# Attention scores per head over four PSUM banks, with VectorE masking all tiles but the first

## The reference, cut to what matters

```python
def xattn(Q, ctx):                          # Q = layernorm(x)
    q, k, v = heads(Q @ Wq.T), heads(ctx @ Wk.T), heads(ctx @ Wv.T)
    s = einsum('nhqd,nhkd->nhqk', q, k) / sqrt(32)
    s = where(padding_mask, s, -inf); s = where(attention_mask, s, -inf)
    a = softmax(s); a = where(isnan(a), 0, a)
    return einsum('nhqk,nhkd->nhqd', a, v).reshape(n, s, 512) @ Wo.T
x = x + xattn(layernorm(x), ctx_1024)
x = x + (layernorm(x) @ W[idx].T + b[idx])  # idx: one expert for each of the 256 positions
```

## Time and profile before

| | |
|---|---|
| median of 3 runs | 872.61 us (872.24 to 873.02) |
| the profiled execution's own time | 871.33 us |
| its span, from first to last instruction | 869.5 us |
| PE busy | 843.0 us, 97% |
| DVE busy | 697.8 us, 80% |
| POOL busy | 630.0 us, 72% |
| ACT busy | 434.9 us, 50% |
| granted TensorE clock, mean | 0.99 of full speed |

### The profile page before, as it was taken

How to read it: one execution, slowest core, us unless ns; L and a number is a source line. 1 busy time by engine, 2 the same in 40 slices (tenths; PEclk the granted TensorE clock), 3 DMA queues, 4 the chain that set the end, 5 groups by cost and what they waited for, 6 DMA issues and landing times. The chain is left out here.

```text
span 869.5 us, 19093 instructions
## 1 busy us (share of the span) xinstructions
PE 843.0 (97%) x6509; PEld 676.7 (78%) x6510; DVE 697.8 (80%) x1021; ACT 434.9 (50%) x762; POOL 630.0 (72%) x826
## 2 busy tenths in 40 slices
PE   8999999999999999999999999999993999999996
PEld 6778887778878888778877888777762788888885
DVE  5988888788888888788888888788778877777774
ACT  5655556565755556555756556555465222222221
POOL 3798778686768668686768668685675677777774
PEclk9999999999999999999999999999996999999998
DMA  9613342524252442524243442522488899999993
GB/s 341 226 43 92 116 136 74 171 74 136 74 157 88 135 135 74 170 77 136 74 154 95 132 133 76 162 83 77 141 270 283 256 282 293 291 281 290 286 293 110
DMA packets 123130, 141.70 MB, mean 163 GB/s; under 512 B 16128, under 2 KB 89376, under 8 KB 120992
## 3 DMA queue, kind: packets, MB, share of 16 engines
q1 hardware_dynamic: 108656, 99.45, 36.5%
q0 software_dynamic: 11360, 35.66, 12.8%
q10 hardware_dynamic: 3024, 5.45, 2.2%
HBM read 90.18 MB, written 51.90 MB: 163 GB/s over the span
## 5 line engine op out<-in xcount | busy, mean ns | idle before, releaser
L1827 PE MATMUL pA<-wf_hl,x_hi 128*128 x560 | 139.2, 391 | 1.8 <-DVE wf_hl L356 1.1
L1827 PEld LDWEIGHTS pA<-wf_hl,x_hi 128*128 128x128 f32 x560 | 105.4, 189 | 24.3 <-issue 2.6
L1111 POOL TENSOR_TENSOR s<-s,row 128x1024 f32<-128x1024 f32 x64 | 121.8, 1903 | 3.1 <-DVE row L1371 3.1
L1768 ACT CAST x_hi<-x2t 128x512 fp32r<-128x512 f32 x70 | 43.5, 621 | 147.1 <-PE pA L1827 136.4
L1519 PE MATMUL pS<-wo_hi,ot_hi 128*128 128x512 f32 x256 | 106.9, 418 | 0.3 <-DVE ot_lo L1375 0.3
L1087 POOL TENSOR_SCALAR y_mom<-y_mom 128x1 f32<-128x1 f32 x64 | 15.9, 248 | 124.9 <-DVE y_mom L1392 123.8
L1519 PE MATMUL pS<-xt_hi,wq_hi 128*128 128x512 f32 x256 | 105.3, 411 | 0.2 <-DVE wq_lo L1412 0.2
L1222 ACT CAST ot_hi<-pA 128x512 fp32r<-128x512 f32 x64 | 37.6, 587 | 128.9 <-PE pA L1622 128.8
L1519 PE MATMUL pS<-wo_lo,ot_hi 128*128 128x512 f32 x256 | 100.9, 394 | 0.0
L1519 PE MATMUL pS<-wo_hi,ot_lo 128*128 128x512 f32 x256 | 100.8, 394 | 0.0
L1519 PE MATMUL pS<-xt_lo,wq_hi 128*128 128x512 f32 x256 | 100.6, 393 | 0.0
(11 more groups left out here) (134 smaller groups left out, 1937.6 us busy)
## 6 DMA issues: line engine op xcount, KB each, us to landing
xq<-x_scratch SPq DMA_DIRECT2D x280, 64.0 KB
xt_raw<-in_x_t SPq DMA_DIRECT2D x16, 1024.0 KB, 6.9
x<-in_x SPq DMA_DIRECT2D x64, 256.0 KB, 3.2
y_scratch<-y_biased SPq DMA_DIRECT2D x64, 256.0 KB, 2.1
x_scratch<-y_normal SPq DMA_DIRECT2D x64, 256.0 KB, 2.9
wf_hl<-in_wf ACTq DMA_DIRECT2D x5, 1024.0 KB, 6.1
ctx_raw<-in_ctx_t SPq DMA_DIRECT2D x32, 128.0 KB, 3.0
wf_hl<-in_wf SPq DMA_DIRECT2D x3, 1024.0 KB, 8.7
```

The lines of the kernel that those rows point to most:

```text
L1111: pool.tensor_tensor(p, p, h.row[:, t % h.c, 3, :].unsqueeze(2).broadcast_to([P, H, BK]), ALU.mult)\
L1827: return pe.matmul(pA[:, r % 2, :], rows[:, r % 2, c * P:(c + 1) * P], w, start=first, stop=last)
```

## The change

Scores are now made head by head. A product takes 32 rows (one head), all 128 positions as weights and the 64 keys of that head; sixteen of them replace the eight. Head `4j + m` sits on rows `32j` to `32j + 31` and goes to bank 2 + j, so that four row groups write four banks. These are 256 columns in each of banks 2 to 5 (`pF`), and thus overlap what is now the second half of `pS` and both banks of `pT`; the projections move to banks 0 and 1. As scores and transposes share banks 4 and 5, PE gets two new waits: `scores(t)` waits for `p_copied` of tile t-2, and `transpose_p(t)` waits until DVE has drained the scores of tile t+1. `kd` loses its zeros, its two memsets and seven of the eight copies of `kt_copy`. Only tile 0 is masked on PE. `scores(t+2)` stands after `project_o(t-1)` in all steps, and in step 0 after the first piece of Q. Three idle products follow `weigh_v` in steps 59 to 62. The route's placing product moves from `pT` to `pA`, since scores now take `pT`'s bank.

```diff
-        self.pe_masks = (0, 1) + tuple(range(self.tiles - 5, self.tiles))
+        self.pe_masks = (0,)
...
-    def scores_late(self, t):
-        return t < self.tiles - 7
-
-    def scores_first(self, t):
-        return self.tiles - 7 <= t < self.tiles - 2
+    def has_scores(self, t):
+        return t < self.tiles - 2
...
-        pS = top.enter_context(nc.psum_tensor("pS", [P, 2, 2 * 512], F32))
-        pT = top.enter_context(nc.psum_tensor("pT", [P, 2, 512], F32))
-        pA = top.enter_context(nc.psum_tensor("pA", [P, 2, 512], F32))
+        banks = top.enter_context(nc.psum_tensor("banks", [P, 8, 512], F32))
+        pS = banks[:, 0:4, :].rearrange("p (r b) n -> p r (b n)", r=2)
+        pT = banks[:, 4:6, :]
+        pA = banks[:, 6:8, :]
+        pF = banks[:, 2:6, 0:HG * BK].rearrange("p j (m k) -> p j m k", m=KC)
...
-        h.kd = sb("kd", [P, 2, h.nb, KC, 2 * BK], F32, st)
+        h.kd = sb("kd", [P, 2, h.nb, KC, BK], F32, st)
...
-            pool.memset(h.kd[:, 1], 0.0).then_inc(zeroed, 1)
...
             def kt_copy(g):
-                if g == 0:
-                    act.wait_ge(zeroed, 2)
                 act.wait_ge(kt_done, g + 1)
-                for j in range(HG):
-                    r = slice(j * DH, (j + 1) * DH)
-                    src = bank("KT", g)[r, :].rearrange("p (c s k) -> p c s k", c=KC, s=2)
-                    for s in range(2):
-                        ins = act.copy(h.kd[r, g % 2, s, :, (j % 2) * BK:(j % 2 + 1) * BK], src[:, :, s, :])
-                ins.then_inc(kt_copied, 1)
+                act.copy(h.kd[:, g % 2], bank("KT", g).rearrange("p (c s k) -> p s c k", c=KC, s=2)).then_inc(kt_copied, 1)
...
-            dve.memset(h.kd[:, 0], 0.0).then_inc(zeroed, 1)
...
-                    if h.scores_first(t):
-                        mask_scores(t + 2)
...
-                    if h.scores_late(t):
+                    if h.has_scores(t):
                         bias_scores(t + 2)
                     ot_low(t)
-                    if h.scores_late(t):
+                    if h.has_scores(t):
                         shift_biased(t + 2)
...
             def scores(t):
                 g, q = divmod(t, h.c)
                 wait(pe, s_drained, t)
+                wait(pe, p_copied, 2 * (t - 1))
...
                 for m in range(KC):
-                    for g2 in range(2):
-                        half = slice(g2 * 64, (g2 + 1) * 64)
-                        mm = pe.matmul(pS[:, 0, g2 * 512 + m * P:g2 * 512 + (m + 1) * P],
-                                       h.qt[half, g % 2, m, q * P:(q + 1) * P], h.kd[half, g % 2, q // 2, m, :],
-                                       start=not biased, stop=not biased or m == KC - 1)
+                    for j in range(HG):
+                        dims = slice(j * DH, (j + 1) * DH)
+                        mm = pe.matmul(pF[:, j, m, :], h.qt[dims, g % 2, m, q * P:(q + 1) * P],
+                                       h.kd[dims, g % 2, q // 2, m, :], start=not biased, stop=not biased or m == KC - 1)
...
             def transpose_p(t):
                 pe.wait_ge(p_ready, t + 1)
+                pe.wait_ge(s_drained, min(t + 2, h.tiles))
...
                     transpose_p(t)
-                    if h.scores_first(t):
-                        scores(t + 2)
                     if t > 0:
                         project_o(t - 1)
-                    if h.scores_late(t):
+                    if t == 0:
+                        project_q(g + 1, 1)
+                    if h.has_scores(t):
                         scores(t + 2)
                     weigh_v(t)
+                    if h.tiles - 6 < t < h.tiles - 1:
+                        keep_clock(pe, 3, free_bank("O", t), w_hi["o"][:, 0, 0:P], w_hi["o"][:, 0, :])
```

More of the change, by code:

```diff
@@ L911, in scores @@
                             half = slice(g2 * 64, (g2 + 1) * 64)
-                            mm = pe.matmul(pS[:, ring, g2 * 512 + m * P:g2 * 512 + (m + 1) * P],
-                                           f.qt[half, m, q * P:(q + 1) * P],
+                            pair = pS[:, ring, g2 * 512:(g2 + 1) * 512].rearrange("p (e m k) -> p m e k", e=2, m=KC)
+                            mm = pe.matmul(pair[:, m], f.qt[half, m, q * P:(q + 1) * P],
                                            f.kd[half, (q // 2) * f.nbk + n, m, :], start=True, stop=True)
@@ L1288, in tiles @@
                         kt_copy(g + 2)
-                    if t + 2 < h.tiles and not h.scores_late(t):
-                        exps(t + 2)
                     if q == 0 and g + 1 < h.groups:
@@ L1383, in residual @@
                 b = h.bank_of("O", t)
-                dve.tensor_tensor(y_sb[:, t % 2, 0:DM], pS[:, 1, b * 512:(b + 1) * 512], h.x_sb[:, t % (2 * h.c), :], ALU.add)\
+                dve.tensor_tensor(y_sb[:, t % 2, 0:DM], pS[:, 0, b * 512:(b + 1) * 512], h.x_sb[:, t % (2 * h.c), :], ALU.add)\
                     .then_inc(added, 1)
@@ L1474, in short_vector @@
             dve.wait_ge(rp, 3)
-            done(dve.tensor_scalar(rows_f[:, 0, :], pT[:, 1, NR:2 * NR], c_batch, None, ALU.add))
-            done(dve.tensor_scalar(rows_f[:, 1, :], pT[:, 1, 0:NR], -float(OOB), float(OOB), ALU.mult, ALU.add))
+            done(dve.tensor_scalar(rows_f[:, 0, :], pA[:, 0, 264 + NR:264 + 2 * NR], c_batch, None, ALU.add))
+            done(dve.tensor_scalar(rows_f[:, 1, :], pA[:, 0, 264:264 + NR], -float(OOB), float(OOB), ALU.mult, ALU.add))
             done(dve.tensor_copy(gather_rows[:], rows_f[:, 0, :]))
@@ L1591, in scores @@
                     r = t % (2 * h.c)
-                    for g2 in range(2):
-                        pe.matmul(pS[:, 0, g2 * 512:(g2 + 1) * 512].rearrange("p (h k) -> p h k", h=H // 2), ident_r[:],
-                                  h.bias[:, r:r + 1, :].broadcast_to([P, H // 2, BK]), start=True, stop=False)
+                    for j in range(HG):
+                        pe.matmul(pF[:, j], ident_r[:], h.bias[:, r:r + 1, :].broadcast_to([P, KC, BK]), start=True, stop=False)
                 for m in range(KC):
-                    for g2 in range(2):
-                        half = slice(g2 * 64, (g2 + 1) * 64)
-                        mm = pe.matmul(pS[:, 0, g2 * 512 + m * P:g2 * 512 + (m + 1) * P],
-                                       h.qt[half, g % 2, m, q * P:(q + 1) * P], h.kd[half, g % 2, q // 2, m, :],
-                                       start=not biased, stop=not biased or m == KC - 1)
+                    for j in range(HG):
+                        dims = slice(j * DH, (j + 1) * DH)
+                        mm = pe.matmul(pF[:, j, m, :], h.qt[dims, g % 2, m, q * P:(q + 1) * P],
+                                       h.kd[dims, g % 2, q // 2, m, :], start=not biased, stop=not biased or m == KC - 1)
                 mm.then_inc(s_done, 1)
@@ L1664, in short_tensor @@
                 n, i = divmod(k, PB)
-                mm = pe.matmul(pT[:, 1, 0:2 * NR].rearrange("p (a n) -> p a n", a=2), place[:, i * P:(i + 1) * P].bitcast(BF16),
+                mm = pe.matmul(pA[:, 0, 264:264 + 2 * NR].rearrange("p (a n) -> p a n", a=2), place[:, i * P:(i + 1) * P].bitcast(BF16),
                                match[:, n, :, i * NR:(i + 1) * NR], start=(k == 0), stop=(k == 2 * PB - 1))
@@ L1680, in tiles @@
                     transpose_p(t)
-                    if h.scores_first(t):
-                        scores(t + 2)
                     if t > 0:
                         project_o(t - 1)
-                    if h.scores_late(t):
+                    if t == 0:
+                        project_q(g + 1, 1)
+                    if h.has_scores(t):
                         scores(t + 2)
                     weigh_v(t)
+                    if h.tiles - 6 < t < h.tiles - 1:
+                        keep_clock(pe, 3, free_bank("O", t), w_hi["o"][:, 0, 0:P], w_hi["o"][:, 0, :])
                     if t == h.tiles - 1:
                         keep_clock(pe, 8, pT[:, 0, :], w_hi["o"][:, 0, 0:P], w_hi["o"][:, 0, :])
+                    if q == 0 and 0 < t and g + 1 < h.groups:
+                        project_q(g + 1, 1)
                     if q == 0 and g + 1 < h.groups:
-                        project_q(g + 1, 1)
                         project_q(g + 1, 2)
@@ L1960 @@
     pad = a["mask_BxS2_bf1"].reshape(B, 2, P).transpose(2, 0, 1)
-    head_order = [g2 * H // 2 + 2 * m + e for m in range(KC) for g2 in range(2) for e in range(2)]
+    head_order = [KC * j + m for m in range(KC) for j in range(HG)]
     rows = np.concatenate([np.arange(h * DH, (h + 1) * DH) for h in head_order])
```

21 lines of the change are left out of this document (10 added, 11 removed).

## The result

| | before | after |
|---|---|---|
| median | 872.44 us (4 runs, 872.24 to 873.02) | 879.43 us (4 runs, 878.72 to 879.77) |
| the profiled execution, its span | 871.33, 869.5 us | 879.77, 878.0 us |
| T1 (transposes of step 1) | 51.13 | 52.33 |
| T57 | 599.91 | 601.06 |
| T57 to T63 | 43.32 | 49.08 |

The change makes the kernel slower by 0.8%: the ratio is 1.008, with a 95% interval of 1.0064 to 1.0096. The difference of the spans, 8.5 us, has three places: 1.15 us are there by T57, 5.8 us come between T57 and T63, 1.6 us after T63.

What follows compares the result with a forecast made beforehand. The prediction took PE to bound attention and the expert layer. Steady steps -0.5, prologue +1.2 and last steps +5.4 gave +6.1 us on the median of 872.6, so 878.7 us, with a range of 873 to 884.

Steps and rivals of the forecast that it cites:

- Scores group: PE's scores products of a tile: eight rounds stay at 0.11 us, set by the weight load; 0.04 us saved a group.
- Waits at q=2: Steady steps with q=2: scores wait for `pt_copy` and start 0.13 us late, in 13 steps, 1.7 us lost.
- the ring: Last steps: add, subtract, exponential, `y_normalise`, `pt_copy`, scores, next add form a closed path; no step under 8.45 us.
- Steady steps in all: Steps 1 to 56: 2.2 us saved in scores, 1.7 lost to waits for `pt_copy`; -0.5 us.
- Prologue: Start, tile 1: DVE's third pass delays `wo_lo` and `normalise_p(1)` on POOL, so transposes of step 1 come 1.2 us later.
- Last steps: Transposes of step 57 to those of step 63: 48.7 us in place of 43.3, +5.4 us.
- the wait for the drained scores: Transposes wait until DVE's add has drained the scores: hidden behind a projection in steady steps, else some 0.7 us.
- After T63: From the transposes of step 63 through the expert layer to the end: same lengths as before, no change.
- the clock's fall before T63: Sign of being wrong: PE's clock falling before the transposes of step 63.
- a rival at a chance of 0.05: PE's clock falls in the last steps because PE stands empty: +4 us, so 883 us; chance 0.05.
- the main case: Whole kernel: 878.7 us, own range 876 to 882, chance 0.73.
- The sum: Whole kernel: -0.5 + 1.2 + 5.4 = +6.1 us, giving 878.7 us, slower by 0.7%.

Runs made afterwards that it cites:

- half_positions: The changed kernel with only positions 0 to 63 of each tile as weights in the scores' products from tile 2 on, the rest left out: 857.62 us.
- double_stream: The changed kernel with each scores product but tile 0's streaming its 64 key columns twice, with the same loads of 128 columns: 885.38 us.
- ynorm_after_copy: The changed kernel with ACT's `y_normalise` moved behind the copies of `pt_copy` from step 5 on: 875.51 us, ratio to before 1.0034.
- before_dve_masks: The kernel before, own banks kept, with masks of tiles 59 to 63 on DVE and their scores behind `project_o`: 878.24 us, ratio to before 1.0067.

## Why the prediction was right

- **Scores group** (0.04 us less): 1.05 us, as forecast, by the load, which half_positions and double_stream show. The Trainium skill, TensorE: Matmul & The Clock Gate (LDWEIGHTS), has P / 1.2 ns for a load; by it 64 columns would be 53 ns, an estimate, and the round measured 58 to 59; 128 would be 107, and measured 111 to 112. The Trainium skill, TensorEngine Tiling (Overview), has up to 4x for 32 rows and up to 2x for 64, as theoretical speedups; the group here gained 4% and not the half that this would give, so for it the measurement decides.
- **Waits at q=2** (+0.13 us a step): such steps went from 11.07 to 11.17 us, which with the 0.04 of the group is 0.15. The signal from ACT to PE takes 0.10 there and 0.14 in the ring, not 0.06. Steady steps in all: -0.05 us from T1 to T57, where -0.5 was forecast; step 2 alone, which I didn't cost, took 0.5 us more than before (11.62 us).
- **Prologue** (+1.2 us): T1 went from 51.13 to 52.33, as forecast, and by the forecast path: POOL began `wo_lo` at 44.13 in place of 42.85, and PE's transposes began 0.05 us after the end of `normalise_p(1)`. T0 scatters by more than this term, so it is read in these two executions alone.
- **Last steps** (+5.4 us): +5.76 in the profiled executions. DVE's step of 57 took 8.91 us and not 9.1. Of the three rings the first took 8.88 us, since ACT was still copying V when its exponential was due (it started at 619.52, the subtract had ended at 619.23); the other two took 8.51 and 8.50, not 8.45. T63 came 49.1 us after T57, not 48.7. That the ring runs through `y_normalise` and `pt_copy` is shown by ynorm_after_copy. What the forecast missed is that the ring isn't the only floor: DVE's own work with its new masks asks for 7.6 us, and the wait for the drained scores stands ready behind it. It didn't matter for the sum, since the longest of three decides, but undoing one part alone returns little: PE's masks gave back 0.7 us between T57 and T63 where I had expected 4, `y_normalise` 2.3 where I had expected 2.6. At the median, masks and order alone cost nearly as much as the whole change (before_dve_masks), so that the size of this term is right for the traces and not shown for the median.
- **After T63** (nothing): +1.6 us. This is the one step that failed. The forecast named the clock's fall before T63 as a sign of being wrong, and it fell twice before T63, at 632.8 and 649.8 us. It was a rival at a chance of 0.05 and a price of +4; in the profiled execution it came with the main case, not in its place, at a price of 1.5. I had named the gaps that go with it, and gave it too little.
- **The sum** (+6.1 us): between medians +7.0 (879.43 - 872.44), between the two profiled executions' spans +8.5 (1.15 + 5.76 + 1.6). Before's profiled execution lies 1.1 us under its median and after's 0.3 over, which is the 1.4 us between the two. That the forecast of 878.7 lies 0.7 us from the median is in part luck: the clock's 1.5 us and the scatter of T0 were not in it.

## What to carry to other kernels

When buffers of consecutive stages come to share a PSUM bank, draw the path from each new wait back to itself through all engines: if it closes, its length is a floor for the step, and it shows only in those steps where nothing longer (here the projections) covers it. For narrow products, count the weight columns that load in each round before the streamed ones: halving the columns of a load gave what halving its rows didn't. Time a filler in the kernel it is meant for; the one that cost nothing measurable in the changed kernel went with a loss of 4 us beside twice as many products.

## What the runs showed of the hardware that had not been expected

- Loads of 64 columns on four row groups and two column halves, eight at once, still follow at 58 to 59 ns a round; a group of 64 such records is then held by their coming, mostly one in 8 to 17 ns, and takes 0.84 us.
- PE's clock fell to half for 3.4 us at a time with gaps of 2.05 and 1.43 us in PE's last steps, with idle products there or without, and stayed full where more of them cut the gaps to 0.92 us at most. ynorm_after_copy has gaps of 1.05, 0.83 and 1.44 us and kept the full clock. In all 14 profiled executions: nine have a gap of 1.94 us or more in these steps, and each of them had a fall before the end of attention; the five whose longest gap is 0.78 to 1.44 us had none.
- PE stood for 1.2 to 3.3 us with no wait in five places of two kernels with 64 records in a scores group, and each time went on 1.3 to 1.5 us after the end of a 16 KB transfer of instructions that had come 11 to 16 us after the one before it.
- The start of step 0 moves by up to 3.2 us between the profiled executions, and is late in those whose clock fell at 7 to 13 us.
